# Edge convolution on one core: transposes of a step stood together, 26 steps picked, first step of stream 1 not gathered

## Chip, cores and metric

One NeuronCore of a Trainium2 chip runs the whole kernel in one launch. The metric is the device time of that launch in microseconds. The kernel before takes 1768.45 us, the median of 3 runs (1766.47 to 1769.26).

## What is computed

6250 nodes with 64 channels, 200000 edges sorted by destination node. Cut to what matters:

```python
xn  = (x - mean) * rsqrt(var + eps) * gamma + beta        # over the nodes
xi, xj = xn[dst], xn[src]                                 # 200000 x 64 each
h   = relu(concat([xi, xj - xi]) @ W1 + b1)               # 128 hidden
msg = h @ W2 + b2                                         # 64
agg = segment_max(msg, dst, 6250); agg = relu(where(isfinite(agg), agg, 0))
out = layernorm(x + agg)
```

The normalisation is folded into the weights, so per edge two products are wanted: one of `x[src]` (weights `w_xs`), and one that depends on the destination alone (a table `a_dram` of 6250 rows, in three bf16 pieces).

## The kernel before

**Streams and steps.** The edges are cut into two overlapping streams (h = 0 and 1) of 100352 edges that run side by side in the two halves of the partitions. Stream 0 begins at edge 0, stream 1 at edge 99648, so they share 704 edges. A step takes 512 edges (`GE`) of each stream; there are 196 steps (`NI`), in 98 windows of two. TensorE, ScalarE (ACT), VectorE (DVE) and GpSimd (POOL) each run a list of instructions unrolled by Python; they meet at semaphores only, and each does its list in order.

**Where x[src] comes from.** For 172 of the steps (`gathered`) POOL fetches the rows with indirect DMAs of 128 rows each, 4 tiles x 2 streams = 8 a step (line 410), into `xs`, a ring of `NX` = 12 slots; TensorE transposes the four 128x128 blocks into PSUM bank `ps_x` (L995), and ACT copies that to `xg` (L565). For the other 24 steps (`picked`: 11, 19, 27, ... 195, every eighth) the rows are not fetched but computed: the node table lies in SBUF as `xtab` (three bf16 pieces, 50 tiles of 125 nodes), DVE makes a one-hot matrix `oh` of each node tile against the 1024 source ids (L780), and TensorE multiplies it (`select`, L977): 3 pieces x 2 streams = 6 matmuls of 512 columns a tile, 50 tiles a picked step, 1200 tiles in all, summed in bank `ps_g`. These tiles are spread over the steps ahead of the picked one, up to 8 a step, by the planner at the top (`want`, `fill`): each step has four places (0 to 3) in TensorE's list where its share is done. An ordinary step has `[2, 2, 1, 1]`, `[2, 2, 2, 1]` or `[2, 2, 2, 2]` tiles, a picked one `[0, 3, 3, 2]`, the one ahead of it what is left. The one-hots lie in a ring of `NOH` = 10; DVE reuses a slot ten tiles later and waits for a semaphore of TensorE that tells that the old tile is read (L773 to L779). DVE makes one-hots up to `AHEAD` = 2 tiles beyond the step it is at.

**A step in TensorE's list** (k, order before): transposes of x for step k (L995), selects of place 0, message matmuls of step k-1 into `ps_m` (L1004), selects of place 1, transposes of the running maxima of step k-2 into `ps_x` too (L1016), the part of the hidden layer from the table (`aw` with the window's one-hot, L1025), the part from `xg` (L1028), selects of place 2, sums of the finished rows of step k-2 (L1043), selects of place 3.

**ACT** in step k: copy to `xg` (L565), copy of the transposed maxima to `rows` (L569), ReLU of the hidden layer (L576, two), the window's one-hot of step k+1 (L538, L542), now and then ids of the next picked step (`node_keys`, L520). **DVE** in step k: running maximum of step k-2 (scan, L832, which waits for `turn_ps`), `pick` (L834), at the end of each group of 7 windows the layer norm (L785 to L814), then the one-hots (L780). **SP** loads the windows. When the last window is done, POOL scatters the last rows (L425).

Of the kernel before, what the change touches and what calls it, by code (L numbers as in the profile page):

```python
# [6 lines left out]
def edge_conv_program(nc, x, src, dst, gamma, beta, W1, b1, W2, b2, out):  # L7
# [38 lines left out]
    PICKED = 24  # L46
# [11 lines left out]
    assert E - S >= 1 and SB % TG == 0 and PICKED * TN % NOH == 0  # L58
# [20 lines left out]
    assert len(picked) == PICKED and tiles == total  # L79
# [7 lines left out]
    with ctx:  # L87
# [28 lines left out]
        step = sb("step", [NW, 2, WE + 1])  # L116
# [66 lines left out]

        res, cen = part[:, :], part_sq[:, :]
# [11 lines left out]
        ps_c = pb("ps_c", [P, GE])  # L196
# [3 lines left out]
        slots_ps = ps_c[:, 0:SL]  # L200
        slots_v = slots_ps.rearrange("p (a n) -> p a n", a=1).to_broadcast([P, TG * 2, SL])
# [11 lines left out]
        sum_v = ps_c[0:ROWS, GE - WB * C:GE].rearrange("p (w c) -> p w c", c=C)  # L213
# [3 lines left out]
        slots_ready, cols_ready = sem("slots_ready"), sem("cols_ready")  # L217
# [28 lines left out]
        turn_ps, run_ready = sem("turn_ps"), sem("run_ready")  # L246
# [143 lines left out]
        def _(pool):  # L390
# [11 lines left out]
            def gather(g):  # L402
# [5 lines left out]
                for t in range(TG):  # L408
                    for h in range(2):
# [26 lines left out]
            with pool.Else():  # L436
                for u in range(NX):
                    pool.wait_ge(rows_in[u], TG * 32)
# [12 lines left out]
        def _(act):  # L451
# [78 lines left out]
            with act.If(windowed == 1):  # L530
# [24 lines left out]
                window_onehot(0)  # L555
                segment = 1
                for k in range(NI + 2):
                    if k < NI:
                        if k in picked:
                            act.wait_ge(segment_ps, picked.index(k) + 1)  # L560
                        else:
                            act.wait_ge(x_ps, gathered.index(k) + 1)
                        if k >= 2:
                            act.wait_ge(hid_ps, k - 1)
                        act.activation(xg[:, k % 2, :], ps_g[:, :] if k in picked else ps_x[:, :], ACT.Copy).then_inc(x_sb, 1)  # L565
                    j = k - 2
                    if j >= 0:
                        act.wait_ge(turn_ps, j + 2)
                        act.activation(rows[:, j % 2, :, 0:C], ps_x[:, :].rearrange("p (t c) -> p t c", c=C),  # L569
                                       ACT.Copy).then_inc(rows_sb, 1)  # L570
                    if k < NI:
                        act.wait_ge(hid_ps, k + 1)
                        if k >= 2:
                            act.wait_ge(turn_ps, k - 1)
# [38 lines left out]
        def _(dve):  # L613
# [22 lines left out]
            dve.memset(xwin[:, :, :], 0.0).then_inc(zeros_ready, 1)  # L636
            dve.sem_inc(g_merged, 1)
            dve.wait_ge(consts_ready, 5)
            dve.tensor_copy(slots_ps, slot_row[:, :]).then_inc(slots_ready, 1)
# [95 lines left out]
            chain(dve.tensor_scalar(order[:, 0:1], dst_r[0:1, 1, 0:1], -1.0, -1.0, ALU.mult, ALU.add))  # L735
# [18 lines left out]
            dve.wait_ge(slots_ready, 1)  # L754
# [6 lines left out]
            with dve.If(windowed == 1):  # L761
# [19 lines left out]

                def norm_sum(n, c0, c1):
# [6 lines left out]
                    dve.tensor_tensor(sum_v[:, c0:c1, :], acc_v[:, c0:c1, 0:C], bias2[:, c0:c1, :], ALU.add).then_inc(end_step, 1)  # L789
# [301 lines left out]
```

## Time and profile before

| | us |
|---|---|
| median of 3 runs | 1768.45 |
| profiled execution, its own time | 1767.39 |
| span of its instructions | 1765.6 |
| PE busy in the span | 1648.7 |
| DVE busy | 1192.8 |
| ACT busy | 965.7 |
| POOL busy | 1316.6 |

The profile is of one execution, and all positions below are microseconds from the start of its span. PE is TensorE, PEld its weight loads. L-numbers are lines of the kernel before. A row of the timeline merges instructions of a kind: start, busy time, engine, line, operation, count, and in brackets how long the engine was idle before it and what ended that. Modelled ends of matmuls overlap the next start, so the time that a piece takes on TensorE is read from start to start.

### The profile page before, as it was taken

To read this page: it belongs to the slowest core of one execution; us is meant where nothing else is said; L and a number is where in the kernel's file an instruction comes from. 1 tells how busy PE (TensorE), PEld (TensorE's weight loads), DVE (VectorE), ACT (ScalarE), POOL (GpSimd) and SP (SyncE) were. 2 spreads that over 40 slices of the span, in tenths; PEclk is the share of its full clock that TensorE was granted. 3 is DMA by queue.
4 is the path that set the end of the run, shared out by engine and by line. 5 is a ranking of instruction groups with operands and counts; after the bars stand their busy time and mean duration, and the time that the engine had idled before them with its cause. 6 is when DMAs were issued, how large, how long until landed. Compare 5 with 4: busy or idle time off the path is not lost. (4 is left out here: it accounts for less than half of the span.)

```text
span 1765.6 us, 37964 instructions
## 1 busy us (share of the span) xinstructions
PE 1648.7 (93%) x13968; PEld 803.4 (46%) x13968; DVE 1192.8 (68%) x1871; ACT 965.7 (55%) x1305; POOL 1316.6 (75%) x1392
## 2 busy tenths in 40 slices
PE   4699999999999999999999999999999999999995
PEld 3444444444444444444444444444444444444442
DVE  6766776766766767667667667676676676766764
ACT  3665555555555455555555555555555555555553
POOL 7777777777777777777777777777777777777773
PEclk8599999999999999999999999999999999999998
DMA  5643234324324333342253243432432524325311
GB/s 129 199 129 96 66 82 108 77 52 118 96 47 123 79 86 94 68 115 69 53 130 85 48 120 82 107 77 65 123 80 53 127 69 102 90 56 118 85 39 24
DMA packets 134675, 157.36 MB, mean 89 GB/s; under 512 B 77570, under 2 KB 79505, under 8 KB 134333
## 3 DMA queue, kind: packets, MB, share of 16 engines
q1 hardware_dynamic: 88684, 109.45, 20.8%
q0 software_dynamic: 44592, 45.31, 15.2%
q8 instruction: 112, 1.84, 0.4%
q14 instruction: 73, 0.60, 0.1%
q10 hardware_dynamic: 1214, 0.17, 0.1%
HBM read 147.05 MB, written 9.39 MB: 89 GB/s over the span
## 5 line engine op out<-in xcount | busy, mean ns | idle before, releaser
L410 POOL DMA_INDIRECT xs<-in_x,src_ix x1376 | 1303.8, 948 | 421.8 <-issue 417.0
L977 PE MATMUL ps_g<-oh,xtab 125*64 125x512 bf16 x7200 | 911.1, 382 | 41.6 <-ACT late L565 34.0
L780 DVE TENSOR_SCALAR oh<-ps_k 125x1024 bf16<-125x1024 bf16 x1200 | 740.0, 682 | 76.2 <-PE ps_x L995 40.0
L977 PEld LDWEIGHTS ps_g<-oh,xtab 125*64 125x64 bf16 x7200 | 364.4, 109 | 557.8 <-issue 213.9
L832 DVE TENSOR_TENSOR_SCAN runmax<-rb,runmax,ps_m 128x512 f32<-128x512 bf16 x196 | 250.7, 1279 | 414.4 <-PE ps_x L1016 398.5
L569 ACT ACTIVATE rows<-ps_x 128x512 f32<-128x512 f32 x196 | 117.1, 597 | 527.9 <-PE ps_x L1016 520.0
L576 ACT ACTIVATE hid<-ps_h,bias 128x512 f32<-128x512 f32 x392 | 247.9, 683 | 179.9 <-PE ps_h L1028 179.9
L542 ACT ACTIVATE late<-late,ones 126x1024 bf16<-126x1024 bf16 x196 | 225.1, 1148 | 6.4
L538 ACT ACTIVATE late<-kb,minus_key 126x1024 bf16<-126x1024 bf16 x196 | 224.6, 1146 | 3.5 <-DMA kb<-keys_dram 3.5
L1028 PE MATMUL ps_h<-late,w_xs 64*128 64x512 f32 x784 | 222.2, 644 | 0.0
L1004 PE MATMUL ps_m<-hid,w 128*64 128x512 f32 x784 | 202.8, 596 | 8.1 <-ACT hid L576 6.6
L1016 PE MATMUL ps_x<-ident,runmax 128*128 128x128 f32 x784 | 128.7, 287 | 6.4 <-ACT late L565 6.3
L1043 PEld LDWEIGHTS ps_acc<-rows,late 128*42 128x42 f32 x3136 | 114.0, 118 | 44.5 <-ACT rows L569 7.9
L1043 PE MATMUL ps_acc<-rows,late 128*42 128x65 f32 x3136 | 122.7, 220 | 1.4 <-ACT rows L569 1.4
L1016 PEld LDWEIGHTS ps_x<-ident,runmax 128*128 128x128 f32 x784 | 82.5, 141 | 89.9 <-issue 87.8
L1025 PE MATMUL ps_h<-late,aw 126*128 126x512 bf16 x392 | 117.6, 381 | 3.8 <-ACT late L542 3.8
L995 PE MATMUL ps_x<-ident,xs 128*128 128x128 f32 x688 | 113.9, 288 | 4.1 <-issue 2.7
L565 ACT ACTIVATE late<-ps_x 128x512 f32<-128x512 f32 x172 | 99.9, 581 | 20.2 <-PE ps_x L995 19.9
L995 PEld LDWEIGHTS ps_x<-ident,xs 128*128 128x128 f32 x688 | 72.8, 142 | 76.1 <-issue 74.2
L1028 PEld LDWEIGHTS ps_h<-late,w_xs 64*128 64x128 f32 x784 | 59.2, 185 | 83.5 <-issue 82.3
L834 DVE TENSOR_TENSOR late<-ps_c,last_key 128x336 f32<-128x336 f32 x196 | 94.5, 482 | 0.0
L1004 PEld LDWEIGHTS ps_m<-hid,w 128*64 128x64 f32 x784 | 54.2, 138 | 43.2 <-ACT hid L576 9.4
(144 smaller groups left out, 381.3 us busy)
## 6 DMA issues: line engine op xcount, KB each, us to landing
kb<-keys_dram SPq DMA_DIRECT2D x98, 504.0 KB
rb<-reset_dram SPq DMA_DIRECT2D x196, 128.0 KB
xs<-in_x,src_ix POOLq DMA_INDIRECT x1376
src_t<-in_src SPq DMA_DIRECT2D x48, 250.0 KB
aw<-a_dram SPq DMA_DIRECT2D x196, 31.5 KB
a_dram<-oh SPq DMA_DIRECT2D x12, 336.0 KB
xwin<-xp_dram SPq DMA_DIRECT2D x196, 10.5 KB
out<-y SPq DMA_DIRECT2D x182, 10.5 KB
```

The lines of the kernel that those rows point to most:

```text
L410: pool.indirect_dma_start(xs[:, u, t, h, :], None, x[:, :], bass.IndirectOffsetOnAxis(ap=src_ix[:, b, q + t, h:h + 1], axis=0))\
L538: act.activation(onehot[:, k % 2, :, :], kb[0:SR, s, :].rearrange("p (h e) -> p h e", h=2)[:, :, i * GE:(i + 1) * GE], ACT.Abs, bias=minus ...
L542: act.activation(onehot[:, k % 2, :, :], onehot[:, k % 2, :, :], ACT.Relu, bias=ones[0:SR, 0:1], scale=-1.0).then_inc(onehot_ready, 1)
L576: act.activation(hid[:, k % 2, h, :], ps_h[:, h, :], ACT.Relu, bias=bias1[:, :]).then_inc(hid_sb, 1)
L780: dve.tensor_scalar(oh[0:PN, n % NOH, :], node_keys_ps, n % TN + 0.5, None, ALU.is_equal).then_inc(oh_ready, 1)
L832: dve.tensor_tensor_scan(runmax[:, j % 2, :], rb[:, s, i * GE:(i + 1) * GE], ps_m[:, :], runmax[:, (j + 1) % 2, GE - 1:GE], ALU.add, ALU.m ...
L977: last = pe.matmul(ps_g[h * C:(h + 1) * C, :], xtab[0:PN, w, t, :], oh[0:PN, n % NOH, h * GE:(h + 1) * GE], start=(t == 0 and w == 0), sto ...
L995: last = pe.transpose(ps_x[:, t * P:(t + 1) * P], xs[:, g % NX, t, :, :].rearrange("p h c -> p (h c)"), ident[:, :])
L1004: last = pe.matmul(ps_m[h * C:(h + 1) * C, :], w2[:, :], hid[:, j % 2, h, :], start=True, stop=True)
L1016: last = pe.transpose(ps_x[:, t * P:(t + 1) * P], runmax[:, j % 2, t * P:(t + 1) * P], ident[:, :])
L1028: last = pe.matmul(ps_h[:, h, :], w_xs[h * C:(h + 1) * C, :], xg[h * C:(h + 1) * C, k % 2, :], start=False, stop=True)
L1043: last = pe.matmul(ps_acc[h * 64:h * 64 + SL, p * C1:(p + 1) * C1], pick[:, j % 2, t * 2 + h, :], rows[:, j % 2, t * 2 + h, :], start=(i = ...
```

## The change

- The transposed maxima get a bank of their own, `ps_r` (that of `ps_c`, which goes). The transposes of x for step k+1 are issued in step k, directly behind those of the maxima of step k-2 and ahead of L1025 (`rows_across`). ACT copies them in step k, so step k+1 finds `xg` ready. The wait for `x_sb` between L1025 and L1028 moves ahead of the transposes.
- A new semaphore `msg_ps` is raised by the message matmuls of each step; DVE's scan waits for it, not for the transposes behind them. The slots of `oh` read at places 2 and 3 are free for DVE at the message matmuls of the next step (before: at the start of the next step); those of place 0 at the message matmuls of the same step.
- 26 picked steps and not 24: 11, 18, 25, 32, 40, ... 191, 7 or 8 apart; 1300 tiles; the last select is in step 189 (before 194). The step ahead of a picked one has `[0, 0, 4, 4]` tiles: it waits at place 2 until ACT has copied `ps_g`. The picked step itself is filled as any other.
- 170 gathered steps. In step 0 stream 1 isn't gathered (its 512 edges lie in stream 0 as well); the slot is zeroed by DVE. That is 1356 indirect DMAs and not 1376.
- The sums of the layer norm and the row of slot numbers, which `pick` compares with, lie in SBUF and not in PSUM.

```diff
-    PICKED = 24
+    PICKED = 26
+    REST = 8
...
         if tiles == (len(picked) + 1) * TN:
-            picked.append(k)
-        want = total * max(k - 1, 0) // (NI - 3) - tiles
+            picked.append(k + 1)
+        want = total * max(k - 1, 0) // (NI - REST) - tiles
...
-        if k in picked:
-            fill.append([0] + [(want + 2 - q) // 3 for q in range(3)])
+        if k + 1 in picked:
+            fill.append([0, 0, (want + 1) // 2, want // 2])
...
-        slots_v = slots_ps.rearrange("p (a n) -> p a n", a=1).to_broadcast([P, TG * 2, SL])
+        slots_v = slot_row[:, :].rearrange("p (a n) -> p a n", a=1).to_broadcast([P, TG * 2, SL])
...
# POOL
-                    for h in range(2):
+                    for h in range(sides(k)):
...
# ACT
                 for k in range(NI + 2):
-                    if k < NI:
-                        if k in picked:
-                            act.wait_ge(segment_ps, picked.index(k) + 1)
-                        else:
-                            act.wait_ge(x_ps, gathered.index(k) + 1)
-                        if k >= 2:
-                            act.wait_ge(hid_ps, k - 1)
-                        act.activation(xg[:, k % 2, :], ps_g[:, :] if k in picked else ps_x[:, :], ACT.Copy).then_inc(x_sb, 1)
+                    if k + 1 in picked:
+                        act.wait_ge(segment_ps, picked.index(k + 1) + 1)
+                        act.wait_ge(hid_ps, k)
+                        act.activation(xg[:, (k + 1) % 2, :], ps_g[:, :], ACT.Copy).then_inc(x_sb, 1)
                     j = k - 2
                     if j >= 0:
-                        act.wait_ge(turn_ps, j + 2)
+                        act.wait_ge(turn_ps, j + 1)
...
+                    if k + 1 in gathered:
+                        act.wait_ge(x_ps, gathered.index(k + 1) + 1)
+                        if k >= 1:
+                            act.wait_ge(hid_ps, k)
+                        act.activation(xg[:, (k + 1) % 2, :], ps_x[:, :], ACT.Copy).then_inc(x_sb, 1)
...
# DVE
                     if n >= NOH:
                         step, place = taken_at[n - NOH]
-                        if place < 2:
-                            dve.wait_ge(turn_ps, max(step, 1))
-                        elif step + 1 in gathered:
-                            dve.wait_ge(x_ps, gathered.index(step + 1) + 1)
+                        if place == 1:
+                            dve.wait_ge(turn_ps, step - 1)
                         else:
-                            dve.wait_ge(turn_ps, step + 1)
+                            dve.wait_ge(msg_ps, step if place == 0 else step + 1)
...
-                        dve.wait_ge(turn_ps, j + 1)
+                        dve.wait_ge(msg_ps, j + 1)
...
# TensorE
+                def rows_across(k):
+                    g = gathered.index(k)
+                    pe.wait_ge(rows_in[g % NX], landed(g))
+                    for t in range(TG):
+                        last = pe.transpose(ps_x[:, t * P:(t + 1) * P], xs[:, g % NX, t, :, :].rearrange("p h c -> p (h c)"), ident[:, :])
+                    last.then_inc(x_ps, 1)
+
+                rows_across(0)
                 for k in range(NI + 2):
-                    if k < NI and k not in picked:
-                        g = gathered.index(k)
-                        pe.wait_ge(rows_in[g % NX], (TG * 32) * (g // NX + 1))
-                        for t in range(TG):
-                            last = pe.transpose(ps_x[:, t * P:(t + 1) * P], xs[:, g % NX, t, :, :].rearrange("p h c -> p (h c)"), ident[:, :])
-                        last.then_inc(x_ps, 1)
-                        select_some(k, 0)
+                    select_some(k, 0)
...
                         for h in range(2):
                             last = pe.matmul(ps_m[h * C:(h + 1) * C, :], w2[:, :], hid[:, j % 2, h, :], start=True, stop=True)
-                        if j == 0:
-                            last.then_inc(turn_ps, 1)
-                    if k in picked:
-                        pe.wait_ge(x_sb, k + 1)
+                        last.then_inc(msg_ps, 1)
                     select_some(k, 1)
                     j = k - 2
                     if j >= 0:
                         pe.wait_ge(run_ready, j + 1)
-                        if k < NI:
-                            pe.wait_ge(x_sb, k + 1)
                         for t in range(TG):
-                            last = pe.transpose(ps_x[:, t * P:(t + 1) * P], runmax[:, j % 2, t * P:(t + 1) * P], ident[:, :])
+                            last = pe.transpose(ps_r[:, t * P:(t + 1) * P], runmax[:, j % 2, t * P:(t + 1) * P], ident[:, :])
                         last.then_inc(turn_ps, 1)
+                    if k < NI:
+                        pe.wait_ge(x_sb, k + 1)
+                    if k + 1 in gathered:
+                        rows_across(k + 1)
...
+                    if k + 1 in picked:
+                        pe.wait_ge(x_sb, k + 2)
                     select_some(k, 2)
```

## Rows read from the trace of the kernel before

**Rows 1.** The page, busy time of TensorE and the clock granted in 40 slices

```profile
PE 1648.7 (93%) x13968; PEld 803.4 (46%) x13968; DVE 1192.8 (68%) x1871; ACT 965.7 (55%) x1305; POOL 1316.6 (75%) x1392
...
PEclk8599999999999999999999999999999999999998
```

**Rows 2.** The page, costliest groups: busy us, mean ns | idle before them and its releaser

```profile
L410 POOL DMA_INDIRECT xs<-in_x,src_ix x1376 | 1303.8, 948 | 421.8 <-issue 417.0
...
L780 DVE TENSOR_SCALAR oh<-ps_k 125x1024 bf16<-125x1024 bf16 x1200 | 740.0, 682 | 76.2 <-PE ps_x L995 40.0
```

**Rows 3.** Timeline, from one start of L1028 to the next, six tiles

```profile
906.63 1.13 PE L1028 MATMUL ps_h<-late,w_xs 64*128 64x512 f32 x4
...
908.82 0.81 PE L977 MATMUL ps_g<-oh,xtab 125*64 125x512 bf16 x6
...
909.56 0.66 PE L995 MATMUL ps_x<-ident,xs 128*128 128x128 f32 x4
...
910.15 1.49 PE L977 MATMUL ps_g<-oh,xtab 125*64 125x512 bf16 x12
...
911.47 1.03 PE L1004 MATMUL ps_m<-hid,w 128*64 128x512 f32 x4
...
912.33 1.46 PE L977 MATMUL ps_g<-oh,xtab 125*64 125x512 bf16 x12
...
913.72 0.66 PE L1016 MATMUL ps_x<-ident,runmax 128*128 128x128 f32 x4
...
914.22 0.60 PE L1025 MATMUL ps_h<-late,aw 126*128 126x512 bf16 x2
...
914.74 1.13 PE L1028 MATMUL ps_h<-late,w_xs 64*128 64x512 f32 x4
```

**Rows 4.** Timeline, the same for a step of eight tiles

```profile
181.18 1.13 PE L1028 MATMUL ps_h<-late,w_xs 64*128 64x512 f32 x4
...
190.60 1.13 PE L1028 MATMUL ps_h<-late,w_xs 64*128 64x512 f32 x4
```

**Rows 5.** Timeline, around the first picked step (11): ACT's chain and TensorE

```profile
162.84 1.13 PE L1028 MATMUL ps_h<-late,w_xs 64*128 64x512 f32 x4
...
164.02 1.26 ACT L576 ACTIVATE hid<-ps_h,bias 128x512 f32<-128x512 f32 x2 [0.91 <-PE ps_h L1028]
...
165.18 1.15 ACT L538 ACTIVATE late<-kb,minus_key 126x1024 bf16<-126x1024 bf16 x1
...
166.35 1.15 ACT L542 ACTIVATE late<-late,ones 126x1024 bf16<-126x1024 bf16 x1
167.41 0.58 ACT L565 ACTIVATE late<-ps_g 128x512 f32<-128x512 f32 x1
...
168.04 2.13 PE L977 MATMUL ps_g<-oh,xtab 125*64 125x512 bf16 x18 [1.62 <-ACT late L565]
...
171.12 1.13 PE L1028 MATMUL ps_h<-late,w_xs 64*128 64x512 f32 x4
```

**Rows 6.** Timeline, layer norm of the first group of windows and TensorE's wait

```profile
211.18 0.62 DVE L785 TENSOR_TENSOR bias<-ps_acc,b2b 106x448 f32<-106x448 f32 x1 [1.70 <-PE ps_acc L1043]
...
215.54 1.49 PE L977 MATMUL ps_g<-oh,xtab 125*64 125x512 bf16 x12 [0.90 <-DVE oh L780]
```

**Rows 7.** Timeline, first and last L1028, POOL's last gather (chain that ended last) and its use

```profile
86.63 2.08 PE L1028 MATMUL ps_h<-late,w_xs 64*128 64x512 f32 x4
...
1727.31 0.94 POOL xs L410
...
1730.44 0.66 PE L995 MATMUL ps_x<-ident,xs 128*128 128x128 f32 x4 [1.41 <-DMA xs<-in_x,src_ix]
...
1742.26 1.13 PE L1028 MATMUL ps_h<-late,w_xs 64*128 64x512 f32 x4
```

**Rows 8.** Timeline ahead of the loop, a DVE operation with two SBUF inputs beside a gather

```profile
46.82 0.41 DVE L705 TENSOR_TENSOR xtab<-late,xtab 125x256 bf16<-125x256 f32 x1
46.95 1.11 POOL L410 DMA_INDIRECT xs<-in_x,src_ix  x1 [0.30 <-issue]
```

More of the change, by code:

```diff
@@ L57, in edge_conv_program @@
     assert C == 64 and HID == P and S <= E < 2 * S and TILES == NB * SB and N == PN * TN and NW <= P
-    assert E - S >= 1 and SB % TG == 0 and PICKED * TN % NOH == 0
+    assert E - S >= 1 and 2 * S - E >= GE and SB % TG == 0 and PICKED * TN % NOH == 0
     total = PICKED * TN
@@ L78, in edge_conv_program, with sides, landed @@
     first_step = [0] + [k + 1 for k in picked]
-    assert len(picked) == PICKED and tiles == total
+    assert len(picked) == PICKED and tiles == total and picked[-1] < NI
+    def sides(k):
+        return 1 if k == 0 else 2
+    def landed(g):
+        return sum(16 * TG * sides(gathered[q]) for q in range(g % NX, g + 1, NX))
     keys_dram = nc.dram_tensor("keys_dram", [NW, 2 * WE], bf16, kind="Internal").ap()
@@ L115, in edge_conv_program @@
         reset = sb("reset", [NW, 2, WE], bf16)
-        step = sb("step", [NW, 2, WE + 1])
+        step_t = sb("step_t", [P, 2, WE + 1])
         order_col = sb("order_col", [NW, 1])
@@ L182, in edge_conv_program @@
             .rearrange("p (s t w c) -> p s t w c", s=NS, t=TG, w=NPC)
+        step = step_t[0:NW, :, :]
+        sums = step_t[:, :, :].rearrange("p h e -> p (h e)")[0:ROWS, 0:WB * C].rearrange("p (w c) -> p w c", c=C)
         res, cen = part[:, :], part_sq[:, :]
@@ L437, in _ @@
                 for u in range(NX):
-                    pool.wait_ge(rows_in[u], TG * 32)
+                    pool.wait_ge(rows_in[u], landed(u))
                 def edge_tile(i, first):
@@ L555, in _ @@
                 window_onehot(0)
+                act.wait_ge(x_ps, 1)
+                act.activation(xg[:, 0, :], ps_x[:, :], ACT.Copy).then_inc(x_sb, 1)
                 segment = 1
                 for k in range(NI + 2):
[L558 to L565 removed]
+                    if k + 1 in picked:
+                        act.wait_ge(segment_ps, picked.index(k + 1) + 1)
+                        act.wait_ge(hid_ps, k)
+                        act.activation(xg[:, (k + 1) % 2, :], ps_g[:, :], ACT.Copy).then_inc(x_sb, 1)
                     j = k - 2
                     if j >= 0:
[L568 to L569 removed]
+                        act.wait_ge(turn_ps, j + 1)
+                        act.activation(rows[:, j % 2, :, 0:C], ps_r[:, :].rearrange("p (t c) -> p t c", c=C),
                                        ACT.Copy).then_inc(rows_sb, 1)
+                    if k + 1 in gathered:
[3 more added lines that the diff above has]
+                        act.activation(xg[:, (k + 1) % 2, :], ps_x[:, :], ACT.Copy).then_inc(x_sb, 1)
                     if k < NI:
@@ L573, in _ @@
                         if k >= 2:
-                            act.wait_ge(turn_ps, k - 1)
+                            act.wait_ge(msg_ps, k - 1)
                         for h in range(2):
@@ L734, in _ @@
             chain(dve.tensor_scalar(order[:, 1:2], order[:, 0:1], -1.0, float(SL - 1), ALU.mult, ALU.add))
-            chain(dve.tensor_scalar(order[:, 0:1], dst_r[0:1, 1, 0:1], -1.0, -1.0, ALU.mult, ALU.add))
+            chain(dve.tensor_scalar(order[:, 0:1], dst_r[0:1, 1, GE:GE + 1], -1.0, -1.0, ALU.mult, ALU.add))
             chain(dve.tensor_tensor(order[:, 2:3], order[:, 0:1], first_f[:, 0, NW:NW + 1], ALU.add))
@@ L796, in norm_sum @@
                     dve.sem_inc(xwin_used, 1)
-                    dve.tensor_reduce(norm[:, 0, c0:c1], sum_v[:, c0:c1, :], AX.X, ALU.add).then_inc(end_step, 1)
+                    dve.tensor_reduce(norm[:, 0, c0:c1], sums[:, c0:c1, :], AX.X, ALU.add).then_inc(end_step, 1)
                     dve.wait_ge(end_step, n * ND + 4)
@@ L1025, in _ @@
                             pe.matmul(ps_h[:, h, :], aw[:, s, h, :], onehot[:, k % 2, h, :], start=True, stop=False)
-                        pe.wait_ge(x_sb, k + 1)
                         for h in range(2):
```

18 lines of the change are left out of this document (8 added, 10 removed).

## Prediction

> **What bounds the kernel now.** I read the page's busy times first, then the costliest groups, then one step of the timeline from start to start, and last the steps that take longer than that one. TensorE is busy 93% of the span at the upper clock level, 2.4 GHz, in all slices but the first two and the last [rows 1]. That alone doesn't settle it: POOL issues its 1376 gathers at one per 0.95 + 0.30 us (1303.8 + 421.8 us in all) with next to no wait on anybody, and its last gather, issued at 1727.31, lands just as TensorE wants it: the only wait for gathered rows worth a name, 1.41 us at 1730.44 [rows 2, 7]. So two chains reach the end together, TensorE's own work and POOL's. A change wins only if it shortens both. This one shortens POOL's and trades pieces of TensorE's.
>
> **TensorE's step, from start to start.** From one L1028 to the next is 8.11 us with six tiles [rows 3] and 9.42 with eight [rows 4]. A tile: twelve matmuls run as six pairs, 1.46 us busy less 0.38 for the tail of the last, so 0.216 a pair and, with three pairs, 0.647 a tile. Then the fixed part of a step is 8.12 - 6 x 0.647 = 4.24. Over the run, first L1028 at 86.63 and last at 1742.26 [rows 7], 195 intervals, 1655.6 us: 195 x 4.24 + 1200 x 0.647 = 1603; less 24 x 0.71 for picked steps, which have no x transposes (0.71 is worked out below), 1586. What is left, 69 us, is stalls:
> - 52 us at the 24 picked steps. The first, step 11, takes 171.12 - 162.84 = 8.28, where its three tiles ask for 4.24 + 1.94 - 0.71 = 5.47: 2.81 too long [rows 5]. The last takes 1.2 too long. ACT's chain does it: after L1028 come two ReLUs, two one-hot operations and the copy of `ps_g`, end to end, and TensorE stands until the copy [rows 5].
> - 10 us where a layer norm delays the one-hots (0.9 us at 215.54, the first of 13 groups [rows 6]), 5 us at two steps where ids came late, and some 2 us at the start and at the last gather.
>
> **The change, part by part.**
>
> *Transposes together.* Before L995 stands one tile that takes 0.74 (908.82 to 909.56) and not 0.647; from L995 to the next select is 0.59, from L1016 to L1025 0.50 [rows 3]. Eight transposes in a row are bounded by what four cost inside one group: 0.66 busy less the 0.33 of the last gives 0.11 each. So a separate group costs 0.09 + 0.59 = 0.68, and 0.02 more in the first select behind it, 0.71; four more in a standing group cost 0.44. The saving is 0.27 a step, the price of going from the selects' half-array matmuls to full ones and back: 195 x 0.27 = **-53 us**. No group in the trace stands directly behind another at full clock, so bounds: nothing saved on entry (0.10 less a step, +20 us) and 0.05 more saved (-10). I take 0.27, since within a group the spacing is even. The wait for `x_sb` that moves ahead is over long before.
>
> *Two more picked steps.* 100 tiles x 0.647 = **+65 us**. Steps without x transposes: before 24 x 0.71 = 17, after 26 x 0.44 = 11: **+6**.
>
> *POOL.* 20 gathers fewer x 1.25 = 25 us, so its last is issued at 1702.5 and landed at 1705.5. From there to the last L1028 are one to two steps of some 5 us, so POOL's chain would allow about 1712 for that L1028 in place of 1742. It is worth only what TensorE's chain lets through: the 1.4 us wait goes. Going early costs nothing, the ring of 12 slots stands between.
>
> *The stall at the picked steps.* It moves to the step ahead, q = p - 1, because now that one has no selects before L1028. There L1025 needs the window's one-hot. ACT's chain from L1028 of q - 1: ReLU starts 1.18 later, the second one-hot operation starts 3.51 later and takes 1.15, 4.66 in all; 0.06 until TensorE starts, 0.53 from L1025 to L1028: 5.25 us at least [rows 5, 3]. TensorE itself needs 4.24 - 0.27 - 0.44 = 3.53 plus 0.647 for each tile at places 2 and 3 of q - 1. The planner gives 0 tiles there for 6 of the picks, 1 for 4, 2 for 12 and 3 for 4, so stalls of 1.72, 1.07, 0.43 and 0: **20 us**. The copy of `ps_g` itself is no longer in the chain: it ends at 5.3, its selects start at 6.3 or later.
>
> *A new wait of DVE.* The four tiles at place 2 of q are tiles 0 to 3 of a segment, place 3 has 4 to 7, place 0 of p has 8 and 9. The first tile at place 1 of p is tile 10, and shares the ring's slot with tile 0, which DVE may overwrite only when the message matmuls of p are done. These stand right ahead of place 1. So the one-hot is made while TensorE waits: the message matmuls are busy 1.03 us, the operation takes 0.68 [rows 3, 2], hand-overs some 0.1, together 1.80, against 0.86 from L1004 to the next select [rows 3]: 0.94. 20 of the 25 segments with tiles behind them have this in full, 4 (seven tiles in q) have 0.29: **20 us**. Queued behind that wait on DVE are the other one-hots and the scan of p - 1; the scan has 2 us to spare. So 52 us of stalls become 40.
>
> *Layer norms.* From L785 to the first one-hot's use by TensorE is 215.54 - 211.18 = 4.36 [rows 6]. In the new order the x transposes (0.68) no longer lie ahead of place 1, and more tiles lie ahead of L1043, so TensorE is there earlier: with [2, 2, 2, 1] it stalls 1.76, with [2, 2, 2, 2] 1.11; over the 13 groups 17 us where 10 were: **+7**. Taking operands from SBUF may give 0.3 back for each; I leave it out.
>
> *The last steps.* Steps 191 to 195 have no tiles, so ACT's 5.25 holds and not TensorE's 3.97: 5 x 1.28 = **+6**. Ids for later picks: the same 5 us as before; the distance from id copy to its use by DVE shrinks from three steps to one, and I bound that by 0 and 10 us.
>
> *Start and tail.* The first two steps, 6.2 us each before, lose the copy of `xg` from ACT's chain, and in the tail the scan no longer waits for four transposes (0.5): **-2**.
>
> **Sum.** -53 + 65 + 6 - 1 - 12 + 7 + 6 - 2 = +16 us. Against the profiled span of 1765.6: 1781.6. The median of the runs stands 2.85 above that span, so 1784.5 us.
>
> **A rule on DVE and POOL.** `pick` (196 times, 0.48 us) now has two SBUF inputs. A DVE operation of that kind ran beside a gather at 46.82, and the gather took 1.11 in place of 0.94 [rows 8]; others there took 0.94 to 0.99. At 0.17 each the 196 would cost POOL 33 us at most, which is about the distance by which its chain is now ahead (1712 against 1758). The Trainium skill (GPSIMD Engine Reference, 8. Key points) says that GpSimd shares its SBUF interfaces with VectorE, with contention against instructions that have two SBUF inputs. By that rule, taken at full length, POOL would become the bound; the trace agrees only that there is a contact, with a tenth of a microsecond.
>
> **Rivals.**
> - *The stalls do not come back (faster).* If tiles are in time at places 1 and 2 of the steps around the pick, because the slot is free earlier than I read it or ACT's one-hot isn't what L1025 waits for, the 40 us go: 1784.5 - 40 = 1744.5. For it: the change takes out of the chain exactly the copy for which TensorE stood 1.62 us [rows 5]. Against it: the order of DVE's waits in the diff. It decides the sign from the point where less than about 24 us of the 40 come back. Chance 0.2, of which half lies above 1755.
> - *DVE's list becomes the bound (slower still).* 740 us of one-hots [rows 2] become 802, in steps that are shorter for the same tiles. If a late scan holds the message matmuls once a segment by its own length, 1.3 us, and the norms cost a further 0.5 each, it is 25 x 1.3 + 7 = 40 us more: 1824. Against: DVE stands idle before half its waits. Chance 0.12.
> - *Grouping gives nothing.* If the entry is paid again between the two groups because a wait stands there, up to the whole 53 us stay: up to 1837, at half 1811. Against: in L1016 to L1025 [rows 3] a wait lies between too and costs nothing to be seen. Chance 0.06.
> - *POOL is the bound* by 196 x 0.48 = 94 us (`pick`'s whole length): its last gather lands at 1800, plus 8 to the last L1028 and 23 of tail, 1834. Rows 8 speak against it. Chance 0.03.
>
> **From this to the numbers.** The forecast has 0.59; within it lie the doubts on 0.94 (down to 0: -20, up to 1.3: +9), on the transposes (+20, -10) and the ids (+10), 1765 to 1803. A difference of 0.2%, 3.5 us, is about what a measurement of this kernel can tell from none. Faster by more: the first rival and a twentieth for the lower end of the forecast, 0.24. Within it: 0.08. Slower: 0.68. The range leaves out the lower half of the first rival and the far ends of the slow ones: 1755 to 1810.
>
> **What would show it.** In the changed profile: L1016 and the x transposes as one run of 0.98 us, once a step, and a step of seven tiles at 8.50 (before 8.77); L1028 to L1028 of 5.25 where `[1, 1, 0, 0]` stands ahead, ended by ACT's L542 counterpart; TensorE idle some 0.9 us for a one-hot behind the message matmuls once per pick; POOL done with its gathers near 1703 and TensorE never waiting for them. The forecast is wrong if TensorE's waits on DVE and ACT sum to under 25 us, or if the run of transposes has a gap in its middle.

## The result and the profile after

| | before | after |
|---|---|---|
| median, us | 1767.46 | 1791.98 |
| profiled execution, its own time | 1767.39 | 1789.88 |
| span of its instructions | 1765.6 | 1788.1 |
| first and last L1028 / L1037 | 86.63 / 1742.26 | 88.13 / 1763.96 |

The changed kernel takes 1.0134 times as long, 95% interval 1.0114 to 1.0154: it is slower by 24 us where 16 were forecast (1784.5 against 1768.45; before is 1767.46 in the table because a fourth run came to the three). Of the changed kernel's four executions one took 6114.01 us and is left out of the ratio, the other three lie between 1789.88 and 1792.23. Lines of the changed kernel: `select` L985, transposes of x L1002, message matmuls L1015, transposes of the maxima L1022, `aw` L1035, `w_xs` L1037, one-hots L788, `pick` L842, gathers L418, the window's one-hot L546 and L550.

Of the page, TensorE's busy time and clock, and the two groups that answer to [rows 1, 2]:

```profile
PE 1667.9 (93%) x14560; PEld 855.1 (48%) x14560; DVE 1246.9 (70%) x1973; ACT 962.1 (54%) x1307; POOL 1310.7 (73%) x1372
...
PEclk7599999999999999999999999999999999999997
...
L418 POOL DMA_INDIRECT xs<-in_x,src_ix x1356 | 1297.8, 957 | 415.4 <-issue 411.1
L788 DVE TENSOR_SCALAR oh<-ps_k 125x1024 bf16<-125x1024 bf16 x1300 | 804.3, 680 | 341.8 <-PE ps_m L1015 340.9
```

Busy time of TensorE rises by 19 us, the span by 22.5. The granted clock is where it was (9 in all slices but the first two and the last). A gather takes 957 ns in place of 948. The busy time alone doesn't tell what was saved and what was lost; the steps do. The timeline of TensorE, an ordinary step of seven tiles, with the transposes now behind each other (against [rows 3]):

```profile
142.40 1.13 PE L1037 MATMUL ps_h<-late,w_xs 64*128 64x512 f32 x4
...
148.03 1.46 PE L985 MATMUL ps_g<-oh,xtab 125*64 125x512 bf16 x12
149.43 0.66 PE L1022 MATMUL ps_r<-ident,runmax 128*128 128x128 f32 x4
149.92 0.60 PE L1002 MATMUL ps_x<-ident,xs 128*128 128x128 f32 x4
150.36 0.60 PE L1035 MATMUL ps_h<-late,aw 126*128 126x512 bf16 x2
150.89 1.13 PE L1037 MATMUL ps_h<-late,w_xs 64*128 64x512 f32 x4
```

From start to start 8.49 us (142.40 to 150.89); seven tiles took 8.76 before. The eight transposes take 0.93, without a gap between the two groups. Next the first picked step (11) and the one ahead of it. The timeline of ACT:

```profile
160.42 1.15 ACT L546 ACTIVATE late<-kb,minus_key 126x1024 bf16<-126x1024 bf16 x1
161.59 1.15 ACT L550 ACTIVATE late<-late,ones 126x1024 bf16<-126x1024 bf16 x1
```

TensorE, the same stretch and on to the end of the picked step:

```profile
158.09 1.13 PE L1037 MATMUL ps_h<-late,w_xs 64*128 64x512 f32 x4
...
162.84 0.59 PE L1035 MATMUL ps_h<-late,aw 126*128 126x512 bf16 x2 [0.60 <-issue]
163.37 1.13 PE L1037 MATMUL ps_h<-late,w_xs 64*128 64x512 f32 x4
...
171.38 1.03 PE L1015 MATMUL ps_m<-hid,w 128*64 128x512 f32 x4
173.21 1.49 PE L985 MATMUL ps_g<-oh,xtab 125*64 125x512 bf16 x12 [0.80 <-DVE oh L788]
...
176.08 1.13 PE L1037 MATMUL ps_h<-late,w_xs 64*128 64x512 f32 x4
```

DVE, the same stretch:

```profile
163.67 0.48 DVE L842 TENSOR_TENSOR late<-slot_row,last_key 128x336 f32<-128x336 f32 x1
172.46 3.68 DVE L788 TENSOR_SCALAR oh<-ps_k 125x1024 bf16<-125x1024 bf16 x6 [8.31 <-PE ps_m L1015]
```

Both stalls of the prediction are there. Ahead of the pick ACT's second one-hot operation ends at 162.74, `aw` starts at 162.84, and the interval of L1037 is 5.28. (The label in brackets is "issue", yet the start follows ACT's end by 0.1: the releaser is inferred.) In the picked step DVE stands 8.31 us, until the message matmuls of 171.38 are done, then makes the one-hot for tile 10 while TensorE stands 0.80.

**All steps, by one rule.** From each interval of L1037 I take 3.97 + 0.647 a tile, less 0.44 where no x transposes are in it; what is left is stall. (3.97 is the forecast's 4.24 - 0.27; it asks for 8.50 where seven tiles take 8.49. Step 195, which has no x transposes either, is counted without the 0.44, as the forecast did.) For before it is the same rule with 4.24 and 0.71. The columns before and after are measured, in us:

| stall | before | forecast | after |
|---|---|---|---|
| at the picks: step ahead + picked step | 52.3 | 20 + 20 | 22.4 + 20.9 |
| layer norms | 9.6 | 17 | 15.7 |
| last five steps | - | 6.4 | 11.9 |
| ids | 5 | 5 | 0 |

### The profile page after: what moved, and what is told of

The parts are those of the page before. It is cut to its first block, busy times and chain, and to the rows that moved or that the text cites. A ratio compares the mean times of both kernels' runs of the same rounds, so it can differ in the third digit from the quotient of the medians.

```text
span 1788.1 us, 39232 instructions
## 1 busy us (share of the span) xinstructions
PE 1667.9 (93%) x14560; PEld 855.1 (48%) x14560; DVE 1246.9 (70%) x1973; ACT 962.1 (54%) x1307; POOL 1310.7 (73%) x1372
## 4 chain that ended last, share of the span: by engine, by line
PE 84%; DVE 5%; ACT 3%; issue 2%; SPq 2%; DMA 1%; POOL 0%; POOLq 0%; DVEq 0%
PE ps_g L985 45%; PE ps_h L1037 11%; PE ps_m L1015 8%; PE ps_r L1022 6%; PE ps_h L1035 5%; PE ps_acc L1054 4%; PE ps_x L1002 4%; DVE oh L788 2%; ACT hid L587 1%; ACT late L550 1%; ACT late L546 1%; SPq L346 1%; SPq L355 0%; DMA out<-y 0%; DMA kb<-keys_dram 0%
## 5 line engine op out<-in xcount | busy, mean ns | idle before, releaser
L418 POOL DMA_INDIRECT xs<-in_x,src_ix x1356 | 1297.8, 957 | 415.4 <-issue 411.1
L788 DVE TENSOR_SCALAR oh<-ps_k 125x1024 bf16<-125x1024 bf16 x1300 | 804.3, 680 | 341.8 <-PE ps_m L1015 340.9
L985 PE MATMUL ps_g<-oh,xtab 125*64 125x512 bf16 x7800 | 935.5, 380 | 30.4 <-DVE oh L788 29.8
L985 PEld LDWEIGHTS ps_g<-oh,xtab 125*64 125x64 bf16 x7800 | 415.7, 109 | 566.9 <-issue 149.5
L575 ACT ACTIVATE rows<-ps_r 128x512 f32<-128x512 f32 x196 | 116.8, 596 | 582.5 <-PE ps_r L1022 575.9
L550 ACT ACTIVATE late<-late,ones 126x1024 bf16<-126x1024 bf16 x196 | 225.0, 1148 | 6.4
L546 ACT ACTIVATE late<-kb,minus_key 126x1024 bf16<-126x1024 bf16 x196 | 224.6, 1146 | 7.1 <-DMA kb<-keys_dram 7.1
L1037 PE MATMUL ps_h<-late,w_xs 64*128 64x512 f32 x784 | 223.2, 646 | 0.0
L1015 PE MATMUL ps_m<-hid,w 128*64 128x512 f32 x784 | 202.7, 595 | 12.7 <-ACT hid L587 10.5
L1035 PE MATMUL ps_h<-late,aw 126*128 126x512 bf16 x392 | 117.9, 382 | 15.6 <-ACT late L550 9.8
L1022 PE MATMUL ps_r<-ident,runmax 128*128 128x128 f32 x784 | 128.5, 286 | 0.0
L1022 PEld LDWEIGHTS ps_r<-ident,runmax 128*128 128x128 f32 x784 | 82.1, 140 | 94.0 <-issue 93.9
L1002 PE MATMUL ps_x<-ident,xs 128*128 128x128 f32 x680 | 103.1, 275 | 6.7 <-ACT late L565 3.9
L1037 PEld LDWEIGHTS ps_h<-late,w_xs 64*128 64x128 f32 x784 | 59.4, 186 | 83.9 <-issue 83.9
L842 DVE TENSOR_TENSOR late<-slot_row,last_key 128x336 f32<-128x336 f32 x196 | 94.7, 483 | 0.0
L1002 PEld LDWEIGHTS ps_x<-ident,xs 128*128 128x128 f32 x680 | 80.4, 143 | 7.9 <-ACT late L565 4.3
L1015 PEld LDWEIGHTS ps_m<-hid,w 128*64 128x64 f32 x784 | 54.5, 137 | 48.4 <-ACT hid L587 15.9
```

Of the source, the lines that this page charges most:

```text
L418: pool.indirect_dma_start(xs[:, u, t, h, :], None, x[:, :], bass.IndirectOffsetOnAxis(ap=src_ix[:, b, q + t, h:h + 1], axis=0))\
L546: act.activation(onehot[:, k % 2, :, :], kb[0:SR, s, :].rearrange("p (h e) -> p h e", h=2)[:, :, i * GE:(i + 1) * GE], ACT.Abs, bias=minus ...
L550: act.activation(onehot[:, k % 2, :, :], onehot[:, k % 2, :, :], ACT.Relu, bias=ones[0:SR, 0:1], scale=-1.0).then_inc(onehot_ready, 1)
L985: last = pe.matmul(ps_g[h * C:(h + 1) * C, :], xtab[0:PN, w, t, :], oh[0:PN, n % NOH, h * GE:(h + 1) * GE], start=(t == 0 and w == 0), sto ...
L1002: last = pe.transpose(ps_x[:, t * P:(t + 1) * P], xs[:, g % NX, t, :, :].rearrange("p h c -> p (h c)"), ident[:, :])
L1015: last = pe.matmul(ps_m[h * C:(h + 1) * C, :], w2[:, :], hid[:, j % 2, h, :], start=True, stop=True)
```

## The experiments

Each kernel is compared with the kernel before in the same series on one chip, whose median was 1768.3 to 1770.7 us except where said. The edits are made to the changed kernel, except in experiment 6. The sizes that follow are given from the stall rule above and from the spans, 1788.1 for after.

**1. The ring slot, alone.** In the planner, for the changed kernel:

```
+        elif k in picked:
+            fill.append([(want + 3) // 4, 0, (want - (want + 3) // 4 + 1) // 2, (want - (want + 3) // 4) // 2])
```

A picked step of eight tiles has `[2, 0, 3, 3]` in place of `[2, 2, 2, 2]`, so nothing wants tile 10 right behind the message matmuls.

> The changed kernel, with the picked step's tiles at places 0, 2 and 3 ([2, 0, 3, 3] in place of [3, 3, 2, 2]); nothing else is altered. Theory of the ring slot: the wait for a one-hot behind the message matmuls goes at all 26 picked steps, which in the trace of the changed kernel is 20.9 us; the stalls at the step ahead (22.4 us) stay. 1792.0 - 20.9 = 1771 us, and picked steps of 12 tiles at 11.7 in place of 12.71. Rival: it is DVE's rate and not the one slot that makes TensorE wait, so the stall goes to place 2 or 3 of the same step: 1790 us, picked steps still near 12.7.

Measured: 1770.12 us, ratio 1.001 (1.0 to 1.002). TensorE at the same picked step:

```profile
163.46 1.13 PE L1039 MATMUL ps_h<-late,w_xs 64*128 64x512 f32 x4
...
171.47 1.03 PE L1017 MATMUL ps_m<-hid,w 128*64 128x512 f32 x4
172.44 0.66 PE L1024 MATMUL ps_r<-ident,runmax 128*128 128x128 f32 x4
...
173.89 1.13 PE L1039 MATMUL ps_h<-late,w_xs 64*128 64x512 f32 x4
```

The interval, now of ten tiles, is 10.43, which is 3.97 + 10 x 0.647 and no more; the stall isn't moved to places 2 and 3. (The expectation's "12 tiles at 11.7" overlooked that two of them go to the next interval.) By the rule the stall at picked steps is -0.2 where 20.9 were, the steps ahead are unchanged at 22.4, and the span is 20.2 us shorter. The ring slot was the cause, and the rival of DVE's rate falls.

**2. Work under ACT's chain, alone.** The last tiles of a segment go to places 2 and 3 of the step that stands two ahead of the pick:

```
+        elif tiles + want == (len(picked) + 1) * TN:
+            fill.append([0, 0, (want + 1) // 2, want // 2])
```

> The changed kernel, with the last tiles of each segment, those of the step that stands two ahead of the picked one, at places 2 and 3; the picked step keeps [3, 3, 2, 2]. Theory of ACT's chain: at the step ahead of the pick TensorE waits for the window's one-hot, 5.25 us from L1037 to L1037, so tiles that stand inside this interval cost nothing until it is full. By the fill lists 19.7 us of stall become 3.8; measured stood 22.4. So 22.4 - 16 = 6 us are left there: 1792.0 - 16 = 1776 us. Rival: the tiles are late there for another reason (ids, DVE's rate), the stall is only moved: 1790 us. Together with the ring slot's 20.9 this should give the 1756.6 us measured with both.

Measured: 1774.19 us, ratio 1.0036 (1.0023 to 1.0048). The stall at the steps ahead falls from 22.4 to 7.4, the picked steps keep 20.9, the norms come to 13.6; span 16.3 us shorter, forecast 16. So ACT's one-hot chain set those steps for the most part, and tiles inside its 5.25 us were free. TensorE of this kernel, with two tiles in the interval that had none:

```profile
156.96 1.13 PE L1039 MATMUL ps_h<-late,w_xs 64*128 64x512 f32 x4
158.02 0.84 PE L987 MATMUL ps_g<-oh,xtab 125*64 125x512 bf16 x6
...
159.15 0.82 PE L987 MATMUL ps_g<-oh,xtab 125*64 125x512 bf16 x6
...
162.25 1.13 PE L1039 MATMUL ps_h<-late,w_xs 64*128 64x512 f32 x4
```

**3. Both.** The two edits together.

> The changed kernel with two differences in the planner, both for its new stalls. A picked step has [2, 0, 3, 3] tiles, none behind the message matmuls; and the step two ahead of a picked one, which has the rest of the segment, has it at places 2 and 3, where it lies in TensorE's list between the L1037 of that step and the L1035 of the next, which waits for ACT's one-hot. 1300 tiles, 26 picks, POOL as in the change. Theory: of TensorE's last L1037 at 1764 in the changed kernel's trace, 20.9 us go at the picked steps and 18 of 22.4 at the steps ahead of them (4 are left, where one or two tiles are too few), so TensorE alone would be there at 1725. POOL's last gather ends at 1716 as before, which allows 1725 too. Then 24 of tail: span 1749, time 1751 us where the kernel before takes 1767. The gain over the changed kernel is 41 us, and TensorE begins to wait for gathered rows in the last steps, which have no tiles. Rival (the stalls only move, DVE's list is the bound): 1785 to 1792.

Measured: 1756.61 us (1755.09 to 1757.25), ratio 0.9933 (0.9916 to 0.9949): 0.7% faster than the kernel before, clear of noise, and faster than the changed one. Picked steps -0.2, steps ahead 7.4, norms 13.7; the span is 35.0 us shorter than after's, and the single edits gave 20.2 + 16.3. It misses the expected 1751 at the end, of which the timeline of SP, POOL, ACT and TensorE:

```profile
1690.07 24.68 SPq L360 DMA_DIRECT2D out<-y  x14
...
1717.33 1.02 POOL L422 DMA_INDIRECT xs<-in_x,src_ix  x1 [0.30 <-issue]
...
1719.39 1.15 ACT L550 ACTIVATE late<-kb,minus_key 126x1024 bf16<-126x1024 bf16 x1 [5.79 <-DMA kb<-keys_dram]
...
1720.51 1.09 PE L1006 MATMUL ps_x<-ident,xs 128*128 128x128 f32 x4 [5.19 <-DMA xs<-in_x,src_ix]
```

Two waits end there at nearly the same time: the window's keys, queued on SP behind 24.68 us of output stores, and POOL's last gathered rows. What binds at the end is POOL's list and SP's, not TensorE's own work.

> The kernel both_fills with REST = 5 and not 8: the selects are spread over three steps more, two steps are left without tiles at the end where five were. In both_fills the steps 191 to 193 took 5.25 us, faster than POOL's 10 us a step and than SP's row of 14 stores, so steps 194 and 195 then stood for the window's keys and for the last rows (7.6 and 2.3 us too long). Theory: the last steps take some 8.5 us, SP and POOL are in time, POOL's last gather (1716, landed 1718) is the bound, the last L1041 stands at 1724 to 1727 in place of 1729: 1753 us. Rival (the total of TensorE's work sets the end and the last steps only shift it): 1757.

This is `both_fills` with `REST = 5`, which spreads the last segment's tiles further. 1756.6 us, ratio 0.9925 (0.9908 to 0.9941): the same, and the number of its rival, 1757. By the stall rule the last five steps fall from 13.7 to 3.9, so the gain at the end is there. But norms rise from 13.7 to 18.1, the steps ahead from 7.4 to 11.4, the rest by 2.9. In part that is cover that is missing: steps ahead with one tile stand 1.15. The larger part is POOL. Its view of waits (us in total, times, longest):

```profile
PE ps_x L1006 <- DMA xs<-in_x,src_ix: 9.8, 5, 3.0
```

Four of these five waits, 9.1 us, lie at steps 156, 170, 178 and 185: TensorE has caught up with the gathers ahead of the end, where `both_fills` waits for rows once, 5.2 us. Moving tiles towards the end took the wait away there and made TensorE meet the gathers earlier.

**4. The grouping undone.** `rows_across(k + 1)` stands ahead of the message matmuls, everything else as changed:

```
                     select_some(k, 0)
+                    if k < NI:
+                        pe.wait_ge(x_sb, k + 1)
+                    if k + 1 in gathered:
+                        rows_across(k + 1)
```

> [...] Theory: in the undisturbed steps of the trace of apart a step of seven tiles takes 8.79 us where it takes 8.49 in the changed kernel, 0.30 more, so 170 x 0.30 = 51 us: 1843 us. Rival (grouping gives nothing): 1792.

Measured: 1828.18 us, ratio 1.0326 (1.0309 to 1.0343). TensorE, a step whose transposes stand apart:

```profile
139.78 1.46 PE L985 MATMUL ps_g<-oh,xtab 125*64 125x512 bf16 x12
141.17 0.66 PE L1002 MATMUL ps_x<-ident,xs 128*128 128x128 f32 x4
141.76 1.08 PE L1019 MATMUL ps_m<-hid,w 128*64 128x512 f32 x4
...
144.06 0.66 PE L1026 MATMUL ps_r<-ident,runmax 128*128 128x128 f32 x4
144.56 0.60 PE L1035 MATMUL ps_h<-late,aw 126*128 126x512 bf16 x2
```

The two groups take 0.59 + 0.50 = 1.09 where the eight took 0.93; two tiles ahead of the first take 1.39 and not 1.29; together with 0.05 behind it that is 0.30 a step: seven tiles take 8.79 in place of 8.49 (72 undisturbed steps each). The expected 1843 took this at all steps. The span grew by 38.5 only: 0.30 shows at the ordinary and the picked steps, while most steps ahead of picks and the last ones stay at ACT's 5.25, and the norm steps come out some 4.5 us shorter in all, since the x transposes lie again in front of the place where TensorE waits for the one-hot. So the grouping works and is worth 38.5 us here, not the 53 that 0.27 at every step would make.

**5. Grouping with the old number of picks.** `PICKED = 24` in place of 26.

> The same kernel as picks_24: the changed kernel with 24 picked steps. Theory: TensorE's chain is 65 us shorter, but POOL has 1372 gathers at 1.26 us, so the last rows land at 1738 and the last L1037 stands near 1745: span 1769, time 1772 us, TensorE waits some 45 us for gathered rows. Rival (TensorE alone is the bound): 1727 us.

Measured: 1772.55 us, ratio 1.0014 (1.0004 to 1.0023), as the theory of POOL had it. Its view of waits (us in total, times, longest):

```profile
PE ps_x L1002 <- DMA xs<-in_x,src_ix: 39.4, 17, 6.0
```

TensorE's timeline near the end of the same kernel:

```profile
1726.98 1.08 PE L1002 MATMUL ps_x<-ident,xs 128*128 128x128 f32 x4 [4.11 <-DMA xs<-in_x,src_ix]
```

TensorE waits 39.4 us, 17 times, for gathered rows (45 were expected). What it saves by the grouping it spends on POOL's 1372 gathers. So neither half of the change pays alone: grouping with 24 picks is capped by POOL, and 26 picks with the groups apart took 1828.18 us in experiment 4.

**6. `pick` from SBUF, alone.** In the kernel before, the one edit:

```
-        slots_v = slots_ps.rearrange("p (a n) -> p a n", a=1).to_broadcast([P, TG * 2, SL])
+        slots_v = slot_row[:, :].rearrange("p (a n) -> p a n", a=1).to_broadcast([P, TG * 2, SL])
```

> The same kernel as before_pick_sbuf: the kernel before with pick's slot numbers in SBUF. In the changed kernel's trace the gathers that lie beside pick are too long by some 8 us in all, those beside the layer norm's sums by some 5. Theory: POOL's last gather comes 8 us later, and the time is 1768 + 7 = 1775 us. First rival (no effect of pick): 1768. Second rival (a full-length block): 1861.

Measured: 1774.9 us, ratio 1.0028 (1.0017 to 1.004). Of its page, the gathers, against 1303.8 and 948 in [rows 2]:

```profile
L410 POOL DMA_INDIRECT xs<-in_x,src_ix x1376 | 1310.3, 952 | 421.9 <-issue 415.9
```

Two contacts, first in POOL's timeline of this kernel:

```profile
502.30 1.27 POOL L410 DMA_INDIRECT xs<-in_x,src_ix  x1 [0.30 <-issue]
...
701.02 0.95 POOL L410 DMA_INDIRECT xs<-in_x,src_ix  x1 [0.30 <-issue]
```

And in DVE's:

```profile
502.27 0.48 DVE L834 TENSOR_TENSOR late<-slot_row,last_key 128x336 f32<-128x336 f32 x1
...
701.83 0.48 DVE L834 TENSOR_TENSOR late<-slot_row,last_key 128x336 f32<-128x336 f32 x1
```

POOL's busy time grows by 6.5 us, its last gather comes 6.6 us later (1733.91 against 1727.31), and the kernel takes 4.3 us more. Which of the two begins first decides. At 701 the gather came first: it takes its 0.95 and `pick` its 0.48; so it is at all 164 places where a pick begins inside a gather. At 502 the gather begins inside the pick and takes 1.27. 76 gathers do so. All but one, which begins 12 ns behind its pick, are longer by what is left of the pick beyond 0.12 us (to within 5 ns; nothing where less is left), up to 0.33 and 4.3 us in all; the other 2.2 us are for the most part 1 to 2 ns on each gather that begins inside no pick. In the kernel before, where `pick` reads PSUM, 81 gathers begin inside a pick and none is longer. The Trainium skill ("SBUF — State Buffer", section "SBUF: two separate sides") says that VectorE with two SBUF inputs and GpSimd take their shared ports exclusively, and that the one that comes second blocks fully, where the GpSimd operation reads SBUF. The trace agrees for a gather that comes second, which stands until the pick ends, but shows no wait of a pick that comes second: 482 ns in 164 of them, 484 in the other 32. So the 196 x 0.48 = 94 us of the full-length block never arise; what counts is how many gathers begin inside a pick, and how late in it.

**7. Runs that couldn't separate.** Five runs came first, on chips where the kernel before itself took 2575.87 us (slot_gap, apart, picks_24, before_pick_sbuf) and 2495.38 us (slot_gap_2).

> The changed kernel, with one difference in the planner: a picked step has no tiles at place 1, right behind the message matmuls; its seven or eight are spread as [2, 0, 3, 3] over places 0, 2 and 3. Same 1300 tiles, same picks. Theory (DVE may overwrite the one-hot slot of tile 0 only once the message matmuls of the picked step are done, and TensorE wants tile 10 at once): the 20.9 us that the 25 picked steps take too long in the changed kernel's trace (0.98 each, 0.33 for four) fall to about 0, DVE makes tile 10 while TensorE transposes. Time 1792 - 21 = 1771 us. Rival (DVE's list as a whole is late, it has 100 one-hots more): the number of one-hots is the same, so the wait moves to place 2 and the time stays at 1792.

2656.81 us, ratio 1.0332 (1.0293 to 1.0371).

> The changed kernel with the transposes of x for step k+1 issued ahead of the message matmuls instead of behind the transposes of the maxima: the two groups stand apart again, all else is the same. Theory: a group apart costs 0.71 us, four more in a standing group 0.44, so 0.27 a step in 170 steps: 1792 + 46 = 1838 us, the same at every gathered step, with the stalls at the picked steps unchanged. Rival (grouping gives nothing, what was saved in a step came from the waits that moved): 1792.

2616.65 us, ratio 1.0129 (1.0065 to 1.0192).

> The changed kernel with 24 picked steps and not 26: 1200 tiles, 172 gathered steps, 1372 indirect DMAs. Theory: TensorE's own chain loses 100 x 0.647 = 65 us, but POOL's, 1356 gathers that end at 1716 in the changed kernel's trace, gets 16 x 1.26 = 20 us longer, so its last rows land at 1738; from there one step and a half (6.5 us) and 24 us of tail: span 1769, time 1772 us, and TensorE waits for gathered rows, some 45 us in all, before none. Rival (TensorE alone is the bound): 1792 - 65 = 1727 us.

2596.53 us, ratio 1.0072 (1.004 to 1.0104).

> The kernel before with one difference: DVE's pick reads the row of slot numbers from SBUF and not from PSUM, so it has two SBUF inputs. Theory: the gathers of POOL, which averaged 1.254 us apart before and 1.263 after the change, lose the same 0.06 us a step here, 12 us over 196 steps; POOL's last gather is what TensorE waits for at the end of the kernel before, so all but the little slack shows: 1767 + 11 = 1778 us. First rival (the slower gathers of the changed kernel come from something else): 1767, gathers at 1.254. Second rival (a full-length block, 0.48 us for each of the 196): 1767 + 94 = 1861.

2572.64 us, ratio 0.9997 (0.9972 to 1.0023).

> [...] Theory: the 20.9 us of the picked steps fall to about 0 and the time is 1771 us where the kernel before takes 1767. Rival (DVE's list as a whole is late): 1792.

2575.91 us, ratio 1.0315 (1.0267 to 1.0362). This is the kernel of experiment 1 once more. From its view of waits (us in total, times, longest; "issue" is a wait for nothing that the profile shows, and "remote" names no engine of the kernel either):

```profile
DVE oh L790 <- remote: 630.5, 97, 9.3
PEld ps_g L987 <- issue: 493.1, 826, 5.2
```

DVE stands 630.5 us and TensorE's weight loads 493.1 us in waits for which the profile finds no releaser in the kernel. The kernel before, unchanged, is 727 to 807 us longer there, so something that isn't in the kernels' text held these executions, and their ratios say nothing on the theories: slot_gap is 3% above before here, twice and clear of noise, and 0.1% above it in experiment 1, and it stands above apart here where it is 58 us below it elsewhere. The granted clock of these executions was 0.86 to 0.92, that of the others 0.96 to 0.98. What held them isn't settled; the queue of instruction packets moved the same 116 packets in 0.3% of 2653.4 us (slot_gap) as in 0.4% of 1788.1 us (after), so its total time hadn't grown. Some undisturbed steps agreed even so: one picked step of ten tiles took 10.43 with the slot free, seven steps of seven tiles 8.79 with the transposes apart.

## Why the prediction was right, and what it missed

*Tile, step and grouping.* 0.27 a step was forecast, 8.76 to 8.49 measured. The named bound "nothing saved on entry" is excluded by experiment 4. The 0.647 a tile holds for the whole range: 6.55 us with four tiles, 8.49 with seven, 9.14 with eight. One reading in it was wrong and did no harm: a transpose takes 0.27 and not 0.33, and the first spacing of a group is 0.17, but the others are the 0.11 that was used, and the second group showed 0.44. That the cost of a separate group comes from the change between half-array and full matmuls is argued, not shown; the runs show the cost.

*The stalls at the picks.* 40 us forecast, 43.3 measured. The step ahead had 22.4 for 20: mostly 5.28 to 5.33 in place of 5.25, and more at four of them that lie behind a layer norm. At step 17 it isn't ACT: DVE's scan is late behind the norm, TensorE waits 1.19 for it, and the step takes 6.23; at 31, 46 and 60 ACT has operations of the norm in its chain, and at 46 the scan is late as well. The late scan that the second rival wanted once a segment shows nowhere else. The picked step had 0.98 for 0.94, 20 times, and 0.33 for 0.29, four times. Experiments 1 and 2 took one each away and found 20.2 and 16.3 us of span, so both were causes and on the path. The first rival (1744.5) asked for them not to come back at all; they did, and even with most of them taken out by the fills the kernel came to 1756.6. In the forecast the two stalls, 40 us, are most of the difference between a gain of 24 us and a loss of 16, so the sign was right for the reason given.

*Layer norms.* 1.76 and 1.11 were forecast for the two kinds of step. The first in the changed kernel with one, DVE and TensorE in the timeline:

```profile
336.25 0.63 DVE L793 TENSOR_TENSOR bias<-ps_acc,b2b 106x448 f32<-106x448 f32 x1 [2.81 <-PE ps_acc L1054]
...
340.59 1.49 PE L985 MATMUL ps_g<-oh,xtab 125*64 125x512 bf16 x12 [1.58 <-DVE oh L788]
```

4.34 from one to the other, 4.36 in [rows 6], and the step is 1.77 too long. Ten of the thirteen steps carry the stall: six with seven tiles 1.76 to 2.00, four with eight 1.12 to 1.25, 15.7 in all for 17. Two others coincide with picked steps and add nothing to their 0.98, and the first, at step 16, shows one step later, in step 17 above.

*What the sum missed.* The span came 6.5 us above the forecast: +3.3 at the picks, -1.3 at the norms, -5 for ids, whose wait didn't return, +5.5 at the last steps, +4.8 at start and tail, and -0.9 spread. That is +13.6 against -7.2, so the sum is closer than its terms; that the wait for ids would go wasn't foreseen, and no run shows why it went. The last steps and the start are one kind of error. After's end, SP's timeline first:

```profile
1726.91 23.28 SPq L356 DMA_DIRECT2D out<-y  x14
```

And SP, ACT and TensorE behind that row:

```profile
1750.24 0.36 SPq L333 DMA_DIRECT2D kb<-keys_dram  x1
...
1753.98 1.15 ACT L546 ACTIVATE late<-kb,minus_key 126x1024 bf16<-126x1024 bf16 x1 [3.57 <-DMA kb<-keys_dram]
...
1756.36 1.03 PE L1035 MATMUL ps_h<-late,aw 126*128 126x512 bf16 x2 [3.79 <-ACT late L550]
...
1757.33 2.08 PE L1037 MATMUL ps_h<-late,w_xs 64*128 64x512 f32 x4
```

SP issues fourteen output stores in 23.28 us and only then the load of the last window's keys. The kernel makes them slow: each store waits for a row number to be loaded (L355), and each pair for the pair before to land (5.8 us in six waits). Before, step 195 was picked, and its tiles stretched these steps over that time; now the steps are 5.25 and the keys come late: step 194 takes 9.36, and behind TensorE's 3.79 us of idle time the `w_xs` matmuls take 2.08 for 1.13, at a granted clock of 0.50 (from 1757.30 to 1758.40), the lower level, 1.2 GHz. I had named ACT as what is late next there and not SP's list. At the start I counted the copy of `xg` that leaves ACT's chain, and not what now stands ahead of L1035 of step 0: the wait for the first such copy, which was said to be over long before, and the transposes of step 1, at the lower level too (granted clock 0.50 from 86 to 89; TensorE's timeline, start of the loop):

```profile
86.23 1.12 PE L1002 MATMUL ps_x<-ident,xs 128*128 128x128 f32 x4 [3.86 <-ACT late L565]
87.14 1.06 PE L1035 MATMUL ps_h<-late,aw 126*128 126x512 bf16 x2
88.13 2.08 PE L1037 MATMUL ps_h<-late,w_xs 64*128 64x512 f32 x4
```

The transposes take 0.91 from start to start, and begin 0.57 later than L1025 did before (85.66). Together the first L1037 is 1.50 later than [rows 7] have it, though -2 was forecast for start and tail.

*POOL.* Its last gather was forecast for 1702.5. POOL's timeline of after:

```profile
1714.91 0.94 POOL L418 DMA_INDIRECT xs<-in_x,src_ix  x1 [0.30 <-issue]
```

1356 gathers, each some 9 ns longer, are those 12 us. The trace says which: 61 gathers that begin inside a pick are longer by 7.3 us in all, 21 that begin inside the layer norm's operations with SBUF operands (L801, L809, L822) by 5.4. Those of the norm, whose sums the change moved to SBUF, stood in no term of the forecast (L822 had two SBUF inputs before, too, and cost 0.5). [Rows 8] fit the reading of experiment 6: that gather begins 0.28 before the end of the operation of 46.82 and takes 0.17 more. The rule on DVE and POOL had it wrong in taking the 0.17 for all 196 picks: 33 us as a bound, 7.3 measured. TensorE never waits for rows in this kernel, so the 12 us were free here. In experiments 3 and 5 it does wait for them, and there such waits should count; no run has those kernels with the operands in PSUM, so that isn't shown.

## What to carry to other kernels

When two engines' chains end together, price a trade against both: here relief for POOL was paid for on TensorE at 65 us and bought nothing until the stalls around it were moved, which was two branches in the planner. A step from which work is taken away falls back on the next chain, here ACT's 5.25 us; put work that can lie anywhere inside that interval, and keep ring reuse one place away from the matmuls that free the slot. At the ends of a loop, read the list of the queue that loads for it too. And an operand that moves from PSUM to SBUF has a price on POOL's list, if POOL issues gathers all the time.

## What the runs showed of the hardware

- Four fp32 transposes of 128x128 in a group of their own between the half-array matmuls cost 0.27 to 0.30 us a step more than four behind another group; the spacing inside a group is 0.11.
- An indirect gather of GpSimd (0.94 us) that begins while VectorE runs an operation with two SBUF inputs is longer by what is left of that operation beyond 0.12 us, up to 0.33 us for one of 0.48 us; one that has begun before it isn't, nor is the operation. With one of the inputs in PSUM there is no such wait (81 gathers). 196 such operations cost 4.3 us by this in one kernel and 7.3 us in the other.
- The kernel before took 1768, 2495 and 2576 us on different chips; in a variant of the changed kernel (2576 us) VectorE stood 630 us in waits that no engine of the kernel ends. No run here shows why.
